# A Strassen-form attention-context kernel: x sums by accumulating transfers, a new order on both vector engines, and a last block in three pieces

## What is computed

```python
q = cond @ Wq.T + bq                      # one row per batch
k = x @ Wk.T + bk;  v = x @ Wv.T + bv
scores = einsum('bhqd,bhkd->bhqk', q / sqrt(32), k)
attn = clip(scores, 0.0, 1.0)
out = x + (attn[..., None] * v) @ Wo.T + bo
```

## Time and profile before

| | before |
|---|---|
| median of three runs | 189.41 us |
| the profiled execution, its own time | 190.13 us |
| its span, first to last instruction | 188.3 us |
| PE / DVE / ACT / POOL busy | 182.8 / 168.8 / 115.6 / 14.7 us |
| matmuls | 799 |
| transferred | 28.09 MB |

### The profile page before, as it was taken

One profiled execution on the slowest core, in us unless ns is written; L12 is line 12 of the kernel. 1 busy time (PEld: TensorE's weight loads), 2 busy tenths in 40 slices (PEclk: granted clock), 3 DMA queues, 4 the chain that ended last, 5 costly groups with the idle time before them and its releaser, 6 DMA issues.

```text
span 188.3 us, 2351 instructions
## 1 busy us (share of the span) xinstructions
PE 182.8 (97%) x799; PEld 148.0 (79%) x799; DVE 168.8 (90%) x184; ACT 115.6 (61%) x158; POOL 14.7 (8%) x21
## 2 busy tenths in 40 slices
PE   8999999899999999999999999999999999999993
PEld 2868788687868888888888888888888888888881
DVE  1799979999999999999899999998897899799752
ACT  4579874786478495753588475852686574775200
POOL 8000000000000001031000010111000010111000
PEclk9999999999999999999999999999999999999999
DMA  5999560005700006279893006279920006289794
GB/s 224 321 375 419 225 257 2 0 0 188 263 0 0 0 0 115 111 124 225 226 420 122 0 0 115 111 129 279 260 115 0 0 0 115 111 136 298 123 375 182
DMA packets 7930, 28.09 MB, mean 149 GB/s; under 512 B 880, under 2 KB 1008, under 8 KB 7792
## 3 DMA queue, kind: packets, MB, share of 16 engines
q1 hardware_dynamic: 6192, 21.67, 30.1%
q0 software_dynamic: 1728, 6.29, 19.6%
HBM read 19.57 MB, written 8.39 MB: 148 GB/s over the span
## 4 chain that ended last, share of the span: by engine, by line
PE 80%; DVE 9%; DMA 7%; issue 2%; SPq 1%; ACT 0%; DVEq 0%
PE bank_y L328 9%; PE bank_y L332 9%; PE bank_y L330 9%; PE bank_x L328 8%; PE bank_x L332 8%; PE bank_x L330 8%; PE bank_z L332 7%; PE bank_z L328 7%; PE bank_z L330 7%; PE score_bank L387 4%; PE score_bank L388 4%; DVE form_lo L820 4%; DMA x_raw<-wv_t 3%; DMA x_raw<-x_t 3%; DVE work L1058 1%
## 5 line engine op out<-in xcount | busy, mean ns | idle before, releaser
L820 DVE TENSOR_TENSOR form_lo<-work,form_hi 128x1024 fp32r<-128x1024 f32 (+1 forms) x38 | 40.3, 1079 | 4.6 <-ACT form_hi L544 4.6
L544 ACT CAST form_hi<-work 128x1024 fp32r<-128x1024 f32 x28 | 29.0, 1051 | 24.5 <-PE score_bank L388 13.2
L579 ACT ACTIVATE work<-bank_y,const 128x512 f32<-128x512 f32 x30 | 20.0, 688 | 10.2 <-PE bank_y L332 10.2
L801 POOL DMA_DIRECT2D work<-x_t x12 | 10.5, 875 | 152.6 <-DVE work L855 145.5
L328 PE MATMUL bank_x<-form_hi,wo_hi 128*128 128x512 f32 x52 | 20.3, 391 | 0.4 <-issue 0.4
L330 PE MATMUL bank_x<-form_lo,wo_hi 128*128 128x512 f32 x52 | 20.3, 390 | 0.0
L332 PE MATMUL bank_x<-form_hi,wo_lo 128*128 128x512 f32 x52 | 20.3, 390 | 0.0
L579 ACT ACTIVATE work<-bank_x,const 128x512 f32<-128x512 f32 x24 | 16.3, 687 | 6.4 <-PE bank_x L332 6.3
L844 DVE SCALAR_TENSOR_TENSOR work<-relu,work 128x1024 f32<-128x1024 f32 x16 | 19.1, 1218 | 0.0
L330 PE MATMUL bank_y<-form_lo,wv_hi 128*128 128x512 f32 x48 | 18.7, 390 | 0.0
L328 PE MATMUL bank_y<-form_hi,wv_hi 128*128 128x512 f32 x48 | 18.7, 390 | 0.0
(11 more groups left out here) (138 smaller groups left out, 381.2 us busy)
## 6 DMA issues: line engine op xcount, KB each, us to landing
x_raw<-x_t SPq DMA_DIRECT2D x16, 512.0 KB, 7.1
out_t<-work SPq DMA_DIRECT2D x14, 512.0 KB, 3.1
work<-x_t POOLq DMA_DIRECT2D x12, 512.0 KB, 5.3
work<-first_t SPq DMA_DIRECT2D x2, 512.0 KB, 3.6
work<-wq_t SPq DMA_DIRECT2D x2, 512.0 KB, 9.2
work<-wk_t SPq DMA_DIRECT2D x2, 512.0 KB, 11.5
work<-wo_t SPq DMA_DIRECT2D x1, 1024.0 KB, 13.8
out_t<-work SPq DMA_DIRECT2D x4, 256.0 KB, 2.0
```

The lines of the kernel that those rows point to most:

```text
L544: nc.scalar.copy(flat(form_hi, kind), raw(kind, phase)).then_inc(hi_ready[kind], 1)
L579: nc.scalar.activation(result_set(phase)[:, q, j * ROWS:(j + 1) * ROWS], of[:, j, :], ACT.Identity, bias=bias[:, tile:tile + 1], scale=sca ...
L801: pool.dma_start(output_set(s)[:, q, :], x_t[s, q], accum_op=ALU.add).then_inc(residual_added[q], 16)
L820: return nc.vector.tensor_tensor(to, of, hi.bitcast(F32), ALU.subtract)
```

## The change

POOL issues T3, T2 and T4 of super-chunks 1 to 3 as transfers from HBM that add into `x_raw` or `x_sum` (`x_t3`, `x_t2`, `x_t4` of s = 1 to 3, nine in all, 512 KB each); their semaphores now count 16 for each. T2's waits for T1's parts, T4's for T2's. They stand in POOL's list among the residuals. `x_t1` stays on DVE and waits for the high part of the T4 before it. `next_x` waits for less: for `x_t1` where it waited for T4's rest, and in the opening for two of four weight sums. Both vector engines' lists are reordered, mostly in the opening, and in the later phases at single places (`hi(T4)` and `hi(T2)` later, `lo(T4)` later, and others alike). On PE, `first_product` of B21 takes the weight rest ahead of the x rest, c's matmul stands ahead of a's, and the wait for c stands ahead of `scores(0, 1)` instead of `scores(0, 0)`. In phase 7, T1 and B22 are computed in three pieces of 512, 256 and 256 columns, the third in a bank of its own (`score_bank[0]`), and block 12 is added and stored in three pieces, block 22 added in two. The core of the diff:

```diff
--- before.py
+++ after.py
...
+LAST_PIECES = ((0, 0, ROWS), (1, 0, ROWS // 2), (1, ROWS // 2, ROWS // 2))
...
-        c_psum = score_bank[0][:, 0:MT * BATCH].rearrange("p (m b) -> p m b", m=MT)
+        c_psum = score_bank[1][:, 3 * P:3 * P + MT * BATCH].rearrange("p (m b) -> p m b", m=MT)
...
+        def last_piece(piece):
+            j, row, width = LAST_PIECES[piece]
+            return score_bank[0][:, 0:width] if piece == 2 else last_bank[:, j, row:row + width]
...
                 if s > 1:
-                    sp.wait_ge(lo_ready[T4], made(T4, VALUES_AT[s - 1]))
+                    sp.wait_ge(x_t1_ready, s - 1)
                 else:
-                    for ready in wv_sum_ready:
-                        sp.wait_ge(ready, 1)
+                    for n in (0, 2):
+                        sp.wait_ge(wv_sum_ready[n], 1)
...
-            for j in range(2):
-                sp.wait_ge(out12_added, LAST + j)
-                sp.dma_start(out_t[3, Q12, :, j * ROWS:(j + 1) * ROWS],
-                             output_set(3)[:, Q12, j * ROWS:(j + 1) * ROWS]).then_inc(stored[Q12], 16)
-            for q, count in ((Q11, SUPERS), (Q22, SUPERS), (Q21, SUPERS + 1), (Q12, SUPERS + 1)):
+            for piece, (j, row, width) in enumerate(LAST_PIECES):
+                at = slice(j * ROWS + row, j * ROWS + row + width)
+                sp.wait_ge(out12_added, LAST + piece)
+                sp.dma_start(out_t[3, Q12, :, at], output_set(3)[:, Q12, at]).then_inc(stored[Q12], 16)
+            for q, count in ((Q11, SUPERS), (Q22, SUPERS), (Q21, SUPERS + 1), (Q12, SUPERS - 1 + len(LAST_PIECES))):
                 sp.wait_ge(stored[q], 16 * count)
...
-                for w, y in ((wv_hi, form_hi), (wv_hi, form_lo), (wv_lo, form_hi)):
+                terms = [(wv_hi, form_hi), (wv_hi, form_lo), (wv_lo, form_hi)]
+                if kind == B21:
+                    terms = [terms[0], terms[2], terms[1]]
+                for w, y in terms:
...
+            def last_pieces(kind, form, grows):
+                operand_ready(kind, LAST)
+                for piece, (j, row, width) in enumerate(LAST_PIECES):
+                    at = slice(j * P, (j + 1) * P)
+                    for k in range(2):
+                        hi, lo = wo_hi[:, form, k, at], wo_lo[:, form, k, at]
+                        x_hi, x_lo = form_hi[:, kind, k, row:row + width], form_lo[:, kind, k, row:row + width]
+                        bank = last_piece(piece)
+                        pe.matmul(bank, hi, x_hi, start=k == 0 and not grows, stop=False, skip_group_check=grows)
+                        pe.matmul(bank, hi, x_lo, start=False, stop=False, skip_group_check=grows)
+                        mm = pe.matmul(bank, lo, x_hi, start=False, stop=k == 1, skip_group_check=grows)
+                    mm.then_inc(done[kind], 1)
...
             pe.wait_ge(a_rows_ready, 1)
             for k in range(KT):
                 mm = pe.matmul(a_psum[:, k, :], a_rows[:, k * P:(k + 1) * P], const[:, C_FOLD:C_FOLD + BATCH * HEADS],
                                start=True, stop=True)
             mm.then_inc(a_done, 1)
-            pe.wait_ge(q_ready, 2)
-            pe.matmul(c_psum, const[:, C_SAME:C_SAME + P], bk_q[:, :, :], start=True, stop=True).then_inc(c_done, 1)
             first_product(banks[0], W22, B22, False, True)
             pe.wait_ge(a_ready, 3)
-            pe.wait_ge(c_ready, 1)
             scores(0, 0).then_inc(score_done, 1)
             product_t1(1)
+            pe.wait_ge(c_ready, 1)
             scores(0, 1).then_inc(score_done, 1)
...
-            product_t1(LAST)
+            wait(pe, out12_added, LAST - 1)
+            last_pieces(T1, S1, False)
             product_t4(LAST)
-            product_b22(LAST)
+            pe.wait_ge(out22_added, LAST + 1)
+            last_pieces(B22, S4, True)
...
-                        T1: (x_t1_ready, s), T2: (x_t2_ready, s), T3: (x_t3_ready, s), T4: (x_t4_ready, s)}[kind]
+                        T1: (x_t1_ready, s), T2: (x_t2_ready, 16 * s), T3: (x_t3_ready, 16 * s), T4: (x_t4_ready, 16 * s)}[kind]
...
             first_hi(T3, Q12)
-            wv_sum_part(S4, 2)
+            first_values(Q11, banks[0], 0)
             first_hi(B22, Q22)
-            first_values(Q11, banks[0], 0)
-            first_values(Q21, banks[1], 2)
             wk_part(0)
             wk_part(1)
             wk_part(2)
             copy_q_rows()
             wk_part(3)
+            first_values(Q21, banks[1], 2)
             wo_part(W11, 0)
+            wv_sum_part(S4, 2)
             wo_part(W12, 1)
-            wo_sum_part(S1, 0)
             wo_part(W22, 3)
             first_values(Q12, banks[2], 4)
+            copy_a_rows()
             hi(T1, 1)
-            copy_a_rows()
+            wo_sum_part(S1, 0)
+            wv_sum_part(S3, 3)
             wo_sum_part(S2, 1)
-            wv_sum_part(S3, 3)
-            hi(T2, 1)
             wo_sum_part(S3, 2)
+            wo_sum_part(S4, 3)
             first_values(Q22, banks[0], 6)
             hi(B11, 1)
             hi(B21, 1)
             round_scores(0, 0)
-            hi(T4, 1)
-            wo_sum_part(S4, 3)
+            hi(T2, 1)
             hi(T3, 1)
             round_scores(0, 1)
             hi(B22, 1)
             copy_b11(1)
             relu_scores(0, 0)
+            hi(T4, 1)
             relu_scores(0, 1)
             copy_u2(1)
             hi(B11, 2)
...
             copy_out21(1)
+            relu_scores(1, 0)
             hi(T2, 2)
-            relu_scores(1, 0)
...
-            for s in range(3):
-                at = OUTPUTS_AT[s]
-                add_residual(s, Q11, out11_added, at)
-                add_residual(s, Q22, out22_added, at)
-                add_residual(s, Q21, out21_copied, 2 * at)
...
+            def x_t3(s):
+                pool.wait_ge(x_t1_ready, s)
+                pool.dma_start(x_raw[:, Q12, :], x_t[s, Q22], accum_op=ALU.add).then_inc(x_t3_ready, 16)
+            def x_t2(s):
+                pool.wait_ge(hi_ready[T1], made(T1, VALUES_AT[s]))
+                pool.wait_ge(lo_ready[T1], made(T1, VALUES_AT[s]))
+                pool.dma_start(x_sum[:, :], x_t[s, Q22], accum_op=ALU.add).then_inc(x_t2_ready, 16)
+            def x_t4(s):
+                pool.wait_ge(hi_ready[T2], made(T2, VALUES_AT[s]))
+                pool.wait_ge(lo_ready[T2], made(T2, VALUES_AT[s]))
+                pool.dma_start(x_sum[:, :], x_t[s, Q21], accum_op=ALU.add).then_inc(x_t4_ready, 16)
+            x_t3(1)
+            x_t2(1)
+            x_t4(1)
+            for s in range(2):
+                residual_11(s)
+                x_t3(s + 2)
+                x_t2(s + 2)
+                residual_22(s)
+                x_t4(s + 2)
+                residual_21(s)
+                residual_12(s)
+            residual_11(2)
+            residual_22(2)
+            residual_21(2)
+            residual_12(2)
         @block.vector
...
+                if s > 1:
+                    dve.wait_ge(hi_ready[T4], made(T4, VALUES_AT[s - 1]))
                 nc.vector.tensor_tensor(x_sum[:, :], x_raw[:, Q11, :], x_raw[:, Q12, :], ALU.add).then_inc(x_t1_ready, 1)
...
+            def last_out22():
+                dve.wait_ge(x_added[Q22], 1)
+                to = output_set(3)[:, Q22, :]
+                apart = len(LAST_PIECES) - 1
+                split = HALF - LAST_PIECES[apart][2]
+                dve.wait_ge(done[T1], 2 * (LAST - 1) + apart)
+                nc.vector.tensor_tensor(to[:, 0:split], last_bank[:, :, :].rearrange("p j n -> p (j n)")[:, 0:split],
+                                        to[:, 0:split], ALU.add).then_inc(out22_added, 1)
+                dve.wait_ge(done[T1], 2 * (LAST - 1) + apart + 1)
+                nc.vector.tensor_tensor(to[:, split:], last_piece(apart), to[:, split:], ALU.add).then_inc(out22_added, 1)
+            def last_out12(piece):
+                dve.wait_ge(done[B22], 2 * (LAST - 1) + piece + 1)
                 dve.wait_ge(x_added[Q12], 1)
-                to = output_set(3)[:, Q12, j * ROWS:(j + 1) * ROWS]
...
-            wv_sum_part(S2, 1)
-            wv_sum(3)
-            wv_sum_part(S4, 2)
             wk_part(0)
             wk_part(1)
             wk_part(2)
             wk_part(3)
+            scale_q()
+            wv_sum_part(S2, 1)
+            wv_sum(3)
+            scale_bk()
+            x_t1(1)
+            wo_part(W11, 0)
+            wv_sum_part(S4, 2)
+            wo_part(W12, 1)
             wo_sum(0)
-            scale_q()
-            x_t1(1)
-            scale_bk()
-            x_t3(1)
-            wo_part(W11, 0)
-            wo_part(W12, 1)
+            lo(T1, 1)
             wo_sum(1)
-            lo(T1, 1)
-            x_t2(1)
-            wo_sum(2)
             fill_a()
             split_a(0)
+            wo_sum(2)
             sum_c()
+            wo_sum(3)
             wv_sum_part(S3, 3)
-            lo(T2, 1)
-            x_t4(1)
             wo_sum_part(S2, 1)
-            wo_sum(3)
```

(5 more changed lines are left out.)

123 lines of the change are left out of this document (55 added, 68 removed).

## The result

| | before | after |
|---|---|---|
| median of six runs each, side by side | 189.25 us | 192.76 us |
| ratio, with its 95% interval | | 1.0191 (1.0132 to 1.025) |
| the profiled execution, its own time | 190.13 us | 192.06 us |
| its span | 188.3 us | 190.3 us |
| start of `scores(0, 0)` | 34.38 | 32.60 |

The changed kernel is slower by 1.9%. Predicted was 186.9 us, between 186.0 and 188.8; the measured time lies outside, and on the other side of before. The opening did give what it was to give: PE is 1.8 us earlier at `scores(0, 0)`. By the last matmul it is 2.3 us later. So 4.1 us are lost between 34 and 187 us, in a stretch where the prediction allowed a stop of 0.3.

What follows compares the result with a forecast made beforehand. PE bounds the 130 us after about 55 us. Terms 0.49 + 0.36 + 0.75 + 0.25 + 0.5 - 0.3 + 0.6 - 0.16 = 2.5 us off the median 189.41 give 186.9 us, range 186.0 to 188.8.

Steps and rivals of the forecast that it cites:

- The opening: Ahead of scores(0, 0): reordered lists close PE's gaps of 0.49, 0.36 and 0.75 us; start moves from 34.38 to about 32.65.
- the landing of T4 in phase 1: T4's transfer, issued at 40.7, takes 6.3 us and lands at 47.0, stopping PE ahead of T3 by 0.3 us.
- Cost 0. T2 and T4 of these phases have more: each is wanted a whole product later.: Later values phases: x_t3's transfer has 1.8 us spare, T2 and T4 more, so the transfers cost PE nothing there.
- the 8.0 row: Profile row of before: a residual transfer that met four loads took 8.0 us; for phase 1's T4, landing at 48.7.
- Rival (a): Phase 1: T4's transfer meets the loads fully, PE stands 2.0 to 2.4 us ahead of T3; 188.8 us, chance 0.18.
- Rival (d): Later values phases: x_t3 queues behind a residual on POOL, PE stops ahead of B21; 191.5 us (190 to 194), chance 0.09.
- Nine instructions fewer on DVE are worth nothing there: After 55 us: PE bounds and DVE works beside it, so taking nine sums off DVE gains 0.
- B11 of phase 2: Start of phase 2, 0.56 us late behind a wo_lo on DVE: moving that back gains 0.5 us.
- The narrow pieces: T1 and B22 at the end: 24 matmuls of 256 columns at 0.12 us replace 12 of 512; 0.16 us lost.
- The tail: Behind the last matmul: shorter last addition (0.27), smaller store (0.25), shorter matmul record (0.1); 0.6 us gained.
- rival (b): Last pieces: the weight load's 0.188 us sets the pace of the narrow matmuls; 188.5 us, chance 0.08.
- Rival (c): Opening: a new wait, as for late wk, wo or x blocks, takes half the gain, 0.8 us; 187.7 us, chance 0.10.

Runs made afterwards that it cites:

- loads_after_t4: Changed kernel, but loads of super-chunks 2 and 3 wait until T4's transfer of the super-chunk before has landed; 188.18 us, 0.9922 of before.
- act_later_1: Changed kernel, but in phase 1 hi(T4, 1) goes behind relu_scores and copy_u2 on ACT, lo(T4, 1) behind two context instructions on DVE; 190.21 us, 1.0003 of before.
- first_only_loads_wait: Changed kernel with only super-chunk 1's three sums by transfer, the others on DVE with before's later lists, super-chunk 2's loads waiting for T4; 187.42 us, 0.9865 of before.
- sums_on_dve: Changed kernel with all nine sums back on DVE, later lists and load waits as before, opening lists and tail new; 189.65 us, 1.0014 of before.
- both_after_t4: Changed kernel, but next super-chunk's loads and residuals 21 and 12 both wait for T4's landing; 187.73 us, 0.9889 of before.
- both_after_t4_again: Changed kernel with loads and residuals 21 and 12 waiting for T4's landing, taken once more on another chip; 188.00 us, 0.9905 of before.
- tail_only: Kernel before with only the last block in three pieces and block 22 added in two; 189.61 us, 1.0019 of before.
- all_quiet: Changed kernel, with loads, residuals 21 and 12, SP's store of block 22 and load of block 12 all waiting for T4's landing; 187.65 us, 0.9898 of before.
- after_again: Changed kernel unchanged, measured and profiled a second time on another chip; 191.97 us, 1.0102 of before.

## Why the prediction was wrong, and where it was right

**The step that failed first: the landing of T4 in phase 1.** The prediction had the mechanism, the place and the limit: T4 held by the loads, ACT's `hi(T4, 1)` ahead of the copies, T3's product waiting. The 2.85 us from the landing to PE's start were exact: 48.15 + 2.85 = 51.0, and PE starts at 51.04. Mis-sized was the landing, 6.3 us, taken between 5.3 and 8.0; it measured 7.1 and 6.5 in two executions of after, and 6.5 in two variants. The stop is 1.7 or 1.0 us, not 0.3. Of the 1.36 us more in the first, 0.8 are the landing (7.1 for 6.3), 0.35 the issue (41.05 for 40.7), and 0.2 that PE wanted T3 at 49.4 and not at 49.6. The argument "three loads and later than the issue" had the facts right, three loads issued from 41.71 on, and drew too little from them: these loads were all that stood between 5.2 and 7.1 (loads_after_t4).

**The step that failed most: "Cost 0. T2 and T4 of these phases have more: each is wanted a whole product later."** This was never worked out. The prediction followed T3's transfer to B21's bank and found 1.8 us spare. For T4 it looked at when T4's product needs the operand, and there it was nearly right: the operand was ready 0.1 us ahead of the wanted start in phase 5 of after. It did not look at what stands behind `hi(T4)` on ACT: a high part, a relu and `copy_u3`, for which T4's own product waits as well, and which end 1.4 us later. In phase 1 it had asked that very question. With the issue at 131.43 as after has it (the prediction had none), the 8.0 row gives a landing at 139.4; from landing to PE's start after has 143.58 - 139.75 = 3.8 us, so PE could not start before 143.2, and wanted to at 142.2. Phases 3 to 5 cost 1.8 us of late starts in one profiled execution of after and 3.8 in the other.

**Rival (a) was the mechanism, counted once.** It gave 2.0 to 2.4 us for phase 1 alone, 188.8. In place of that came 1.0 to 1.7 us there, and further stops of the same kind in phases 3 and 5. Rival (d) was the only one on the right side in time (190 to 194), with a mechanism that is real but small: ahead of B21 PE was late once, by 0.88 us, in one of two profiled executions of after. What was missing was a rival that carries (a) to all three values phases: 186.9 + 1.9 + 2 x 2.2 = 193.2. That this is near the 192.76 measured is partly luck: it has 6.3 us of stops, where the traces show 3.7 and 5.1, and it keeps the opening's gain at 1.8 us.

**The trace of before showed more of this contention than was read from it.** Of its twelve accumulating transfers one met four loads (8.0). But the longest, 8.4 us, issued at 129.35, had a store and one load beside it, issued at 126.57 and 127.00, and a second store from 130.17: nearly the company of T4 in phase 5. With the change the nine sums come at set points of each values phase, when SP's queue is busy too; the DMA share of 98 to 148 us is 0.70 in after. The Trainium skill (DMA: Bandwidth & Descriptors, Queues, rings and completion order) says that each engine turns between its queues packet by packet. A T4 transfer at 5.1 to 5.4 us with nothing of SP's beside it and 6.5 to 9.4 with loads agrees with that. The Trainium skill's figure for one transfer (DMA: Bandwidth & Descriptors, Anatomy of one DMA), an estimate of 3.2 us for 512 KB from its 2.0 us plus the bytes at 436 GB/s, does not agree: the shortest accumulating one of any run took 5.0.

**The opening was right in its end and wrong in its worth.** `scores(0, 0)` was forecast at 32.65 and came at 32.60, and the gaps closed by the steps given. But the gain was read against one execution, with 34.38, and subtracted from a median that belongs to an earlier start. With 0.7 us between that execution and the median of 189.41, the median's start is near 33.7 (an estimate, by the differences 190.13, 189.88 and 34.38, 34.10), and the opening's gain 1.1 rather than 1.8 us there; beside medians of 190.0 and 190.2 it is 1.6 to 1.8. The prediction named the difference between execution and median, and then did not charge it. Nor is the new start one value: 32.60 and 32.52 in the two executions of after, up to 33.13 in act_later_1 with the same opening.

**"Nine instructions fewer on DVE are worth nothing there": right, and right to be limited to after 55 us.** first_only_loads_wait shows it for six of them. For the three ahead of 55 us the opposite holds: with them back on DVE, sums_on_dve loses 2.1 us of late starts. The prediction put the opening's gain down to the new order alone; it needs the three transfers of super-chunk 1 as well, to be kept past 44 us.

**B11 of phase 2.** Taken as 0.5 of 0.56 gained; 0.22 of a late start remain (54.12), so 0.34. DVE had stood 2.25 us for `hi(T4, 1)` three instructions ahead of B11's rest, so part of the 0.22 may be the stop's. Where T4 landed early it is 0.22 (both_after_t4), 0.14 (both_after_t4_again), or under 0.12 (loads_after_t4).

**The narrow pieces: right. The tail: nearly.** The end of after, PE:

```profile
180.90 0.28 PE L454 MATMUL score_bank<-form_hi,wo_hi 128*128 128x256 f32 x1
181.02 0.28 PE L455 MATMUL score_bank<-form_lo,wo_hi 128*128 128x256 f32 x1
...
187.04 0.28 PE L456 MATMUL score_bank<-form_hi,wo_lo 128*128 128x256 f32 x1
```

The pace is 0.12, so rival (b) falls: the weight load's record of 0.188 does not set it. From the last start to the end of the span it is 3.61 us in before, 3.22 in after and 3.09 in tail_only: 0.38 to 0.52 gained where 0.6 was taken, less 0.16 for the pace; the last addition, of 256 columns, takes 0.42 as forecast. What remains, 0.2 to 0.4 us, is about the edge of tail_only's interval (0.3 us faster at best), so the measured times do not show it.

**Rival (c)** did not come: no new wait in the opening.

**The sum, put right.** Without any stop the forecast puts the last start at 184.71 - (0.49 + 0.36 + 0.75 + 0.25 + 0.5) + 0.16 = 182.5. first_only_loads_wait has 182.53 without a late start and all_quiet 182.61 with one of 0.2, at ratios of 0.9865 and 0.9898, 187.42 and 187.65 us. loads_after_t4, without one too, has 183.14, its `scores(0, 0)` being at 33.06. The arithmetic of PE's stream was sound, for an opening as in the execution read; 3.7 to 5.1 us of stops were missing from it.

**What stays open.** Why the same contention costs 3.7 us in one execution of after and 5.1 in another, and how the packets of the two queues meet in time, no run here separates. Whether loads held back, with `hi(T4)` behind the copies in all three phases, would bring more was not tried; neither was `hi(T4)` behind the copies in phases 3 and 5 with the loads free, where after_again's operand would still be 0.3 late.

## What to carry to other kernels

When a vector sum becomes a transfer, the saved engine time is worth only what that engine holds up, and the price is a wait whose length depends on all traffic beside it; work it out for every phase in which the transfer stands, not for the tightest, and list what is queued behind the waiting instruction rather than when its own operand is needed. A transfer on which a compute engine waits should have the queues to itself: one wait that starts uncritical loads after it turned this change from 1.0 to 1.9% slower to 0.8% faster. Read gains of an opening from several executions, since a late load there can be most of the gain.
